# An attention and feed-forward kernel: the three bf16 parts of K and Q made by TensorE and ScalarE from one fp32 transpose

## The reference

```python
def attention(Q, K, V):                   # K = V = ctx_1024
    scores = einsum('bhqd,bhkd->bhqk', q, k) * 0.25
    return einsum('bhqk,bhkd->bhqd', softmax(scores, -1), v)
def ffn(x, w_gate, w_up, w_down):
    # fp4_linear: x and w rounded blockwise (16) to an fp4 grid, then multiplied
    return fp4_linear(silu(fp4_linear(x, w_gate)) * fp4_linear(x, w_up), w_down)
x = x + attention(layernorm(x), ctx_1024, ctx_1024)
x = x + ffn(layernorm(x), w_gate, w_up, w_down)
```

## Time and profile before

| | us |
|---|---|
| median of 3 runs | 637.24 (634.64 to 638.73) |
| the profiled execution | 639.48 |
| its span, first to last instruction | 637.7 |
| mean granted TensorE clock | 0.989 of full speed |

### The profile page before, as it was taken

One profiled execution on the slowest core, in us unless ns is written; L12 is line 12 of the kernel. 1 busy time (PEld: TensorE's weight loads), 2 busy tenths in 40 slices (PEclk: granted clock), 3 DMA queues, 4 the chain that ended last, 5 costly groups with the idle time before them and its releaser, 6 DMA issues.

```text
span 637.7 us, 13644 instructions
## 1 busy us (share of the span) xinstructions
PE 559.7 (88%) x3780; PEld 343.7 (54%) x3780; DVE 536.4 (84%) x1186; ACT 353.4 (55%) x656; POOL 434.6 (68%) x530
## 2 busy tenths in 40 slices
PE   1479999999999999999888999999999999999996
PEld 1235545555554554555546665665665665666664
DVE  1598999999999999986578889889889889889863
ACT  1226778777777777777635355354354354354341
POOL 7787788878788888723256766766766766766740
PEclk9999999999999999999998999999999999999997
DMA  7834443444434444310000000000000000000000
GB/s 233 187 101 134 134 131 113 125 118 133 123 109 121 118 117 125 100 52 3 1 0 10 9 18 16 8 16 16 8 16 16 8 16 14 10 16 8 17 17 25
DMA packets 43797, 40.61 MB, mean 64 GB/s; under 512 B 4728, under 2 KB 43512, under 8 KB 43768
## 3 DMA queue, kind: packets, MB, share of 16 engines
q1 hardware_dynamic: 43768, 40.26, 22.3%
HBM read 10.55 MB, written 4.19 MB: 23 GB/s over the span
## 4 chain that ended last, share of the span: by engine, by line
DVE 45%; PE 25%; issue 18%; ACT 4%; DVEq 3%; POOL 2%; DMA 1%; SPq 1%; ACTq 0%; POOLq 0%
DVE MF L573 8%; DVE QS L763 7%; PE PV L906 6%; PE MX L888 5%; PE SC L874 5%; DVE hmax L773 4%; DVE hinv L641 3%; DVE KS L791 3%; PE T L810 2%; DVE hinv L645 2%; ACT QS L521 2%; PE SC L988 2%; PE T L860 2%; DVE stats L581 2%; DVE QS L719 1%
## 5 line engine op out<-in xcount | busy, mean ns | idle before, releaser
L573 DVE TENSOR_REDUCE MF<-MX 128x2 f32<-128x512 f32 x256 | 168.6, 678 | 19.6 <-PE MX L888 19.0
L482 ACT ACTIVATE P<-SC 128x512 f32<-128x512 f32 x256 | 146.6, 607 | 22.1 <-PE SC L874 20.0
L888 PE MATMUL MX<-KS,QS 96*128 96x256 bf16 x512 | 104.9, 290 | 19.3 <-DVE MF L573 15.6
L988 PE MATMUL SC<-KS,QS 128*128 128x256 f32 x384 | 93.8, 395 | 17.2 <-ACT QS L537 17.2
L874 PE MATMUL SC<-QS,KS 98*128 98x256 bf16 x512 | 100.7, 279 | 0.5 <-ACT P L482 0.5
L988 PEld LDWEIGHTS SC<-KS,QS 128*128 128x128 f32 x384 | 72.0, 194 | 42.7 <-ACT QS L537 33.8
L432 POOL TENSOR_TENSOR QS<-QS 128x256 f32<-128x256 f32 (+1 forms) x47 | 48.4, 1029 | 56.9 <-ACT QS L532 35.8
L906 PE MATMUL PV<-P,VA 128*32 128x256 f32 x1024 | 82.0, 393 | 0.7 <-ACT P L482 0.4
L888 PEld LDWEIGHTS MX<-KS,QS 96*128 96x128 bf16 x512 | 46.9, 101 | 43.7 <-DVE MF L573 34.3
L874 PEld LDWEIGHTS SC<-QS,KS 98*128 98x128 bf16 x512 | 38.3, 99 | 57.0 <-ACT P L482 36.2
L432 POOL TENSOR_TENSOR KS<-KS 128x704 f32<-128x704 f32 x16 | 26.9, 1681 | 40.9 <-ACT KS L532 40.9
(11 more groups left out here) (109 smaller groups left out, 1112.8 us busy)
## 6 DMA issues: line engine op xcount, KB each, us to landing
KS<-KP SPq DMA_DIRECT2D x96, 128.0 KB, 2.4
QS<-QP SPq DMA_DIRECT2D x96, 128.0 KB, 2.4
X<-in_x SPq DMA_DIRECT2D x16, 256.0 KB, 2.9
C<-in_ctx SPq DMA_DIRECT2D x16, 256.0 KB, 3.1
out<-KS SPq DMA_DIRECT2D x16, 128.0 KB, 1.7
out<-QS SPq DMA_DIRECT2D x16, 128.0 KB, 1.7
W<-in_L_ffn_w_down SPq DMA_DIRECT2D x1, 704.0 KB, 8.0
W<-in_L_ffn_w_gate SPq DMA_DIRECT2D x1, 640.0 KB, 5.0
```

Of the source, the lines that this page charges most:

```text
L482: nc.scalar.activation(P[g % 2][:, j, :, :], SC[h % 3][:, :, :], ACT.Exp, scale=0.25).then_inc(exp_done, 1)
L573: nc.vector.tensor_reduce(MF[st.slot(off, 2)][:, :, h:h + 1], MX[h % 2][:, :, :], AX.X, ALU.max, negate=True).then_inc(mx_done, 1)
L888: last = nc.tensor.matmul(MX[h % 2][:, q, :], QS[r][0:PROD, h, q * 128:(q + 1) * 128], KS[r][0:PROD, h, :], start=True, stop=True)
L988: last = nc.tensor.matmul(DP, HT[r][:, c, :], WDT[:, c, :], start=(c == 0), stop=(c == NT - 1))
```

## The change

- POOL's two splits go. For K it only makes an fp32 copy KN in the order by parity (two instructions of 128x256, the source and form of L364 but with fp32 output). Q needs none: QN is already in that order.
- PE transposes KN (QN) in fp32 into one PSUM bank, four transposes that open an accumulation (`flip`). ACT copies the bank to bf16: that is part 0. PE then multiplies part 0 by a negated bf16 identity and adds it to the bank (`rest`, one matmul of 512 columns), ACT copies part 1, PE subtracts it, ACT copies part 2. K uses TA, Q uses TB.
- In the slots: PE K at (0,0), (0,3), (1,2) and Q at (1,3), (2,2), (3,0); ACT K at (0,1), (1,0), (1,2) and Q at (2,0), (2,2), (3,1). ACT's abs of the weights goes from (0,1) to (0,0) and its copy of the second PV half from (0,2) to (0,3).
- The addition of epsilon goes from DVE (0,2) to POOL, behind the KN copies.
- The transposed maxima go to TA, so PE's `maxima` waits for DVE's first `output`; the second `outputs` goes from (2,3) to (3,0) and waits for `maxima_out`, which goes from DVE (2,2) to (2,3). DVE's first denominators and output are both at (2,1), the second ones at (3,1), were (2,2).
- PE's K transposes wait for the previous step's second `output` (o_norm), since both use TA.

```diff
             def attention_step(st):
                 if st.has(LEAD):
                     r, rc = st.slot(LEAD, 2), st.slot(LEAD, RING)
                     pool.wait_ge(loaded[rc], st.turn(LEAD, RING, 32))
-                    pool.wait_ge(k_tr, st.times(LEAD - 2, 2, 2))
-                    pool.wait_ge(q_parts, st.times(LEAD, 1))
+                    pool.wait_ge(k_tr, st.times(LEAD, 3))
                     gate(pool)
-                    split(lambda q: by_parity(C[rc][:, q, :]), KB[r], 0, k_parts, st)
+                    for q in range(QT):
+                        nc.gpsimd.tensor_scalar(KN[:, q, :, :, :], by_parity(C[rc][:, q, :]), 1.0, 0.0,
+                                                ALU.mult, ALU.add).then_inc(kn_ready, 1)
+                    pool.wait_ge(stats_seq, st.times(LEAD, 4, 4))
+                    gate(pool)
+                    nc.gpsimd.tensor_scalar(ve[r][:, :], mv[:, :, 1], EPS, None, ALU.add).then_inc(ve_ready, 1)
                     pool.wait_ge(ve_ready, st.times(LEAD, 1, 1))
...
-                if st.has(LEAD):
-                    r = st.slot(LEAD, 2)
-                    pool.wait_ge(qn_ready, st.times(LEAD, QT, QT))
-                    pool.wait_ge(q_tr, st.times(LEAD - 2, 2, 2))
-                    pool.wait_ge(k_parts, st.times(LEAD, 1, 1))
-                    gate(pool)
-                    split(lambda q: QN[:, q, :, :, :], QB[r], 5, q_parts, st)
...
-            def part_out(parts, n, tr, out_sem, st):
+            def part_out(parts, bank, n, tr, out_sem, st):
-                act.wait_ge(tr, st.times(LEAD, 2, 1 + n // 2))
+                act.wait_ge(tr, st.times(LEAD, 3, n + 1))
...
-                nc.scalar.activation(parts[:, n, :], (TA16[:, 0:512], TA16[:, 512:], TB16[:, 0:512])[n],
-                                     ACT.Copy).then_inc(out_sem, 1)
+                nc.scalar.activation(parts[:, n, :], bank, ACT.Copy).then_inc(out_sem, 1)
...
+            def flip(bank, src):
+                for e in range(2):
+                    for q in range(QT):
+                        at = e * S + q * 128
+                        last = nc.tensor.matmul(bank[:, at:at + 128], src[:, q, e, :, :].rearrange("p d a -> p (d a)"),
+                                                ident[:, :], start=(at == 0), stop=False, is_transpose=True,
+                                                skip_group_check=True)
+                return last
+            def rest(bank, part, last):
+                return nc.tensor.matmul(bank, negidentb[:, :], part, start=False, stop=last, skip_group_check=True)
+            def keys(st, n):
+                if n == 0:
+                    pe.wait_ge(kn_ready, st.times(LEAD, QT, QT))
+                    pe.wait_ge(o_norm, st.times(-1, 2))
+                    flip(TA, KN).then_inc(k_tr, 1)
+                else:
+                    pe.wait_ge(k_out, st.times(LEAD, 3, n))
+                    rest(TA, KP[st.slot(LEAD, 2)][:, n - 1, :], n == 2).then_inc(k_tr, 1)
+            def queries(st, n):
+                if n == 0:
+                    pe.wait_ge(qn_ready, st.times(LEAD, QT, QT))
+                    pe.wait_ge(q_out, st.times(LEAD, 3))
+                    flip(TB, QN).then_inc(q_tr, 1)
+                else:
+                    pe.wait_ge(q_out, st.times(LEAD, 3, n))
+                    rest(TB, QP[st.slot(LEAD, 2)][:, n - 1, :], n == 2).then_inc(q_tr, 1)
             def maxima(st):
                 pe.wait_ge(m_parts, st.times(1, 1, 1))
...
+                if st.has(-1):
+                    pe.wait_ge(o_norm, st.times(-1, 2, 1))
...
             def outputs(st, q):
...
+                if q == 1 and st.has(1):
+                    pe.wait_ge(mt_ready, st.times(1, 1, 1))
```

More of the change, by code:

```diff
@@ L6 @@
 bf16 = mybir.dt.bfloat16
-int32 = mybir.dt.int32
 ALU = mybir.AluOpType
@@ L119, in program @@
         QN = sb("QN", [128, QT, 2, DK, H // 2])
-        REST = sb("REST", [128, QT, 2, DK, H // 2])
-        KB = [sb(f"KB{r}", [128, 3, QT, 2, DK, H // 2], bf16) for r in range(2)]
-        QB = [sb(f"QB{r}", [128, 3, QT, 2, DK, H // 2], bf16) for r in range(2)]
+        KN = sb("KN", [128, QT, 2, DK, H // 2])
         KP = [sb(f"KP{r}", [128, 3, 512], bf16) for r in range(2)]
@@ L496, in attention_step @@
                         exp(st, g, j)
-                        if (g, j) == (0, 1) and st.has(LEAD - 1):
+                        if (g, j) == (0, 0) and st.has(LEAD - 1):
                             act.wait_ge(w_scaled, st.times(LEAD - 1, 1, 1))
@@ L596, in normalise @@
                 dve.wait_ge(rstd_ready, st.times(LEAD, 1, 1))
-                dve.wait_ge(q_parts, st.times(LEAD, 1))
+                dve.wait_ge(q_tr, st.times(LEAD, 3))
                 nc.vector.tensor_scalar(QN[:, q, :, :, :],
@@ L839, in maxima @@
             def maxima(st):
                 pe.wait_ge(m_parts, st.times(1, 1, 1))
-                if st.has(LEAD):
-                    pe.wait_ge(k_out, st.times(LEAD, 3, 3))
-                else:
-                    pe.wait_ge(q_out, 3 * B)
-                    pe.wait_ge(mt_ready, st.times(1, 1))
+                pe.wait_ge(k_out, st.times(LEAD, 3, 3) if st.has(LEAD) else 3 * B)
+                if st.has(-1):
+                    pe.wait_ge(o_norm, st.times(-1, 2, 1))
                 for q in range(QT):
-                    last = nc.tensor.transpose(TB16[0:2 * H, q * 128:(q + 1) * 128],
+                    last = nc.tensor.transpose(TA16[0:2 * H, q * 128:(q + 1) * 128],
@@ L926, in attention_step @@
                         max_scores(st, g, j)
-                        if (g, j) == (1, 1) and st.has(LEAD):
-                            keys(st, 0)
-                        if (g, j) == (1, 1) and st.has(LEAD):
-                            keys(st, 1)
+                        for n, at in enumerate(((0, 0), (0, 3), (1, 2))):
+                            if (g, j) == at and st.has(LEAD):
+                                keys(st, n)
+                        for n, at in enumerate(((1, 3), (2, 2), (3, 0))):
+                            if (g, j) == at and st.has(LEAD):
+                                queries(st, n)
                         if (g, j) == (2, 0) and st.has(-1):
```

91 lines of the change are left out of this document (18 added, 73 removed).

## The result

Eight runs of each kernel on one chip gave a median of 639.56 us after (638.36 to 640.49) and 635.61 before (634.02 to 638.73): ratio 1.0059, 95% interval 1.0039 to 1.0079. The change makes the kernel slower, by 0.6%. That is inside the 1% that the prediction called "same", but clear of no change, and the forecast had been none. The three runs of before that the prediction had gave 637.24; with eight the median is 1.6 us lower.

A forecast was written before the change was run, and what follows sets the result against it. No single bound: PE and DVE take turns in the attention half. Profiled 639.48 - 2.3 (start) + 2.6 (11 steps) = 639.8; the median is 2.2 lower, 637.5; with small tail gains 637.0 us, range 630 to 645.

The forecast's parts named there:

- the start: Before the steady steps: Q's last issue near 19.4, landing about 24.3; in all -2.3 us, bounds 0 and -4.
- steps 1 to 11: Attention steps between the flips of steps 1 and 12: 17.4 us against 17.16, 11 x .24 = +2.6 us.
- the tail: Last attention steps: small gains there take the forecast from 637.5 to 637.0 us.
- The order decides: Chain from KN ready through the late second output and POOL's addition to the next KN: 17.4 us a step.
- The `rest` product at .22: PE's four added products of 512 bf16 columns a step cost .22 us each, .88 together.
- The subtraction: DVE's subtraction of the maxima, slot (2,0): falls from 1.10 towards 0.19 us, slipping in with .15 to spare.
- The slower rival: DVE slot (2,0): the subtraction waits for POOL's whole second weight operation, +.65 a step, 644 us; chance .20.
- The rival that the start gives nothing: At the start the weight loads pace it, so nothing is gained: 639.3 us; chance .17.
- Steps -1 and 0: Step -1 keeps some .2 us of gain; in step 0 small gains and the new output wait offset, 0.
- The first rival: PE becomes the bound if KN is ready when PE comes: 16.4 us a step, 626 us; chance .18.
- two DVE instructions, .85 and .9: DVE, each step: the epsilon instruction goes, -0.85 us, and the subtraction of the maxima shortens, about -0.9.
- that sum (3.7 against 2.67 us): Product (3,1) to KN ready takes 3.7 us; PE's own work to the flip takes 2.67.

The follow-up runs named there:

- Experiments 1 and 2: experiment 1 (625.3 us), and the changed kernel with POOL's addition of the second half of item t-2 put behind the KN copies (628.49 us).
- experiment 7: The changed kernel with K's pieces two slots later, and POOL also doing the old split of Q with results unused: 634.07 us.
- Experiment 3: The changed kernel with PE's wait for the rows of ones moved from ahead of all its work to the first scores: 642.25 us.
- experiment 5: The changed kernel with SP's loads of items 2 and 3 issued behind item 0's stacks instead of ahead of them: 639.13 us.
- the five kernels above: The changed kernel and four runs on it, with old load order and new K path; first maximum product at 27.66, 28.06, 26.85, 27.18 and 27.02 us.
- experiment 10: The kernel before, with the loads of items 2 and 3 issued behind item 0's stacks: 637.45 us.
- experiment 1: The changed kernel with the KN flip two slots later and the first `rest` one slot later: 625.3 us.
- Experiments 6 and 7: The changed kernel with K's pieces two slots later, and epsilon's addition back on DVE at slot (0,2) (624.11 us); and experiment 7 (634.07 us).
- experiment 9: Maxima put ahead of outputs, against the changed kernel with K later, POOL's second addition behind KN and loads behind stacks (621.3 us): 626.22 us.

## Why the prediction was right or wrong

The forecast was no change, 637.0 against 637.24 us; measured was +3.95 (639.56 against 635.61). Its terms, beside the stretches of the result:

| term | predicted | measured |
|---|---|---|
| the start, up to the statistics of step 1 | -2.3 | +1.4 - 1.7 = -0.3 |
| steps 1 to 11 | +2.6 | +4.4 |
| the tail | about -0.5 | -0.5 |

Two steps of the working failed, about equally: the landing of Q in the start, and the gain of steps 1 to 11, whose mechanism was right and whose size was not. The miss at the start would be 1.7 larger without a gain in step 0 that nobody had foreseen; that is luck.

*The order decides (right).* The chain from the flip to the next flip was worked out at 17.40 and measured 17.47. (One link of it is 0.06 too long: 10.64 and .21, .33 and .22 give 11.40, not 11.46.) PE's idle time at the flip was to be 1.0 and is 0.89, the wait ahead of `maxima` .45 and is 0.40, the KN copies 1.23 and are 1.23. Experiments 1 and 2 remove the wait from either end and gain 1.34 and 1.06 us a step.

*The `rest` product at .22 (right in what it occupies).* Its rows are 0.38 us long, but they overlap the next product as those of 256 columns do: from the rest at 158.48 to the next scores at 158.70 it is .22. The source view:

```profile
L779 PE MATMUL T<-KP,negidentb x23: 379/379/380, 67.7 to 260.2; 128*128 128x512 bf16 x23
```

*The subtraction (right, narrowly).* It took 0.19 and started 0.11 us ahead of POOL's second weight operation, where the prediction had .15. The slower rival, that it would meet POOL, did not come in the changed kernel, but it is real: experiment 7 shows its size.

*"It holds for the 11 periods", +2.6 (a term mis-sized).* Measured +4.4. The prediction took 17.16 for all eleven steps of before, but the first of them, from 67.33 to 83.67, is only 16.34; after, it is 17.40. That is 0.8 of the miss. In that step of before POOL had no addition to do ahead of its split of K, the split was over in time, and epsilon took 0.16 us on DVE; in the next step it took 0.95:

```profile
69.08 0.16 DVE L591 TENSOR_SCALAR ve<-mv 128x2 f32<-128x2 f32 x1
...
85.41 0.95 DVE L591 TENSOR_SCALAR ve<-mv 128x2 f32<-128x2 f32 x1
```

The other 1.0 is the ten steps behind it, 17.51 on average (the first of them 17.80) where 17.40 was predicted.

*The start, -2.3 (the step that failed).* The prediction let Q land 4.9 us after a last issue at 19.4, so at 24.3, as it had after one at 21.43. The last issue came at 20.2, since PE's first flip waited for the rows of ones, and it landed at 27.6, 7.4 us later. The landing time is set by what stands ahead in the queue: it grew from 4.97 to 7.4 as the issue moved forward. The sentence "the DMA queue is already full of weight loads" stood in the same paragraph and was not carried through. Experiment 3 (issue 1.35 sooner, no gain) and experiment 5 (1 MB less ahead of it, 3.6 us sooner) show it. The rival that the start gives nothing named the mechanism; what came was +1.4 to the statistics of step -1, of which 1.2 is the later landing. Why it landed later than before, and not just no sooner, stays open; the five kernels above scatter by 1.2 us themselves. The Trainium skill, DMA: Bandwidth & Descriptors, section Queues, rings and completion order, says that on each DMA engine descriptors are consumed in ring order and that one issuing engine has one ring on each; by that rule Q lands when what SP issued ahead of it on the same DMA engines is done. The trace agrees: with 1 MB less ahead of it, Q landed 2.9 to 3.3 us after its issue and not 5.7 to 7.4.

*Steps -1 and 0, costed at about nothing (wrong by 1.7).* The gain is in step 0, 14.9 us against 17.0; step -1 is 0.4 longer. In the changed kernel the products of step 0 go over to their full rate at 53.2 (rows of 0.63 us for a pair until 52.44, 0.38 from 53.23), 4.6 us after the first scores; in the kernel before the full rate came at about 57.5, 9.8 us after them. Four microseconds more at half the rate cost some 2 us of work at the full one (an estimate from these rows), which is the size of the gain. The column of the granted clock reads 1.00 throughout in both; the spacing of the rows tells that the rate doubled, as between 1.2 and 2.4 GHz. From the first scores to the change of rate PE was busy almost without a gap in both; in the kernel before twelve bf16 transposes stood in that stretch (53.4 to 54.8). In experiment 10 the products reach the full rate at 48.6, then PE is mostly idle from 51.0 to 52.1 (busy 0.21 of 1.10 us), and from 52.1 to 55.4 they are back at half rate, this time with a granted clock of 0.50 in the column. No run separates what sets the moment of the rise.

*The first rival, PE as the bound,* was priced at 16.4 a step and 626. With the wait taken away (experiment 1) the kernel has 16.13 and 625.3. The condition was the one named: KN had to be ready when PE comes. That the total agrees within 1 us is partly luck: the step is 0.27 shorter than priced, some 3 us in eleven, and the start that the price included, 2.3 us, did not come. What the prediction missed is that the condition needed no faster copies, only two slots.

*What POOL's unloading is worth.* The prediction gave it to two DVE instructions, .85 and .9. Experiments 6 and 7 confirm both as durations: 0.93 becomes 0.16, 0.19 becomes 1.04 again. A third was missed: the copy of the maxima to bf16, 0.16 before, takes 0.29 after and ends at 162.05, when POOL's first weight operation (161.22, 0.79 us long) is over. The Trainium skill, GPSIMD Engine Reference, section 1 Specifications, says that POOL shares its SBUF interfaces with VectorE and names contention with DVE instructions of two SBUF inputs; the trace agrees for the subtraction, which has two. Epsilon and the copy have one, and no run tells why they are held.

## What to carry to other kernels

Work moved off a loaded engine gives back nothing if the consumer is moved forward by more than the producer gains: write the chain from the last input of the moved piece to the first instruction that waits for it, across the end of the step, and compare it with the waiting engine's own time between the two points. Here that sum (3.7 against 2.67 us) told of a wait, and moving the flip by two slots turned the loss into a gain (two changed lines, 2.5% off the changed kernel). And a DMA's time to landing read in a crowded stretch must not be added to another issue time; ask what stands ahead of it in the queue. Last, before a wait is called a wait, count the records: here a missing row made 0.40 us look like 0.62, and experiment 9 was built on it.

## What was not expected of the hardware

Landing times of the same six DMAs of 128 KB were 2.9 to 3.3 us with 1 MB less ahead of them and 5.7 to 7.4 with it. An instruction of DVE on two elements a partition took 0.16 us in one step and 0.95 in another of the same kernel. In the long cases DVE's small instruction ends with the instruction that POOL is at: epsilon at 155.02 and POOL's at 155.01, the subtraction at 161.55 and 161.51 (both before), and at 124.74 and 124.70 in experiment 7. And the rate of the products in step 0 doubled 5.2 us sooner after the first scores in one kernel than in the other, under the same granted clock of 1.00.
